# A Mamba and mixture-of-experts block on one core: two buffers for the experts' input, x1 stored early, the gated expert sum accumulated onto it in memory, and a new table of places

## The reference

```python
mod = (_silu(L0_c) @ L0_wmod).reshape(L0_c.shape[0], 6, 1, -1)
sa, ca, ga, sb, cb, gb = (mod[:, 0], ..., mod[:, 5])
ga = (2 * (ga >= 0) - 1) * jnp.maximum(jnp.abs(ga), 0.25)      # gb likewise
h = _layernorm(x) * (1 + ca) + sa
x = x + ga * _L0_attn_ref(h, ...)          # this sum is x1 in the kernel
h = _layernorm(x) * (1 + cb) + sb
x = x + gb * _L0_ffn_ref(h, ...)

def _L0_attn_ref(x, ...):
    h = _rmsnorm(x, norm_w)
    xi, z = split(h @ in_proj_w.T, 2)               # 512 and 512 features
    xi = silu(causal_depthwise_conv(xi, 4 taps) + bias)
    dt, Bm, Cm = split(xi @ x_proj_w.T, [16, 32])   # 16, 16 and 16
    delta = softplus(dt @ dt_proj_w.T + dt_proj_b)
    s = s * exp(delta_t * A) + delta_t * Bm_t * u_t # for each token; 512 x 16 states
    y_t = einsum('bds,bs->bd', s, Cm_t)
    y = (y + u * D) * silu(z)
    return y @ out_proj_w.T + x

def _L0_ffn_ref(x, ...):                            # 16 routed experts, 4 of them per token, and a shared one
    g = sigmoid(x @ gate_w.T); top 4 of 16, normalised -> combine
    routed = sum over e of (silu(x @ e_win[e]) * (x @ e_vin[e]) * combine[e]) @ e_wout[e]
    shared = silu(x @ ws_in) * (x @ vs_in) @ ws_out
    return shared + routed
```

## Time and profile before

| | |
|---|---|
| median of 3 runs | 2980.88 us (2977.16 to 2983.09) |
| profiled execution | 2980.19 us, span in the trace 2978.4 us |
| mean granted clock of TensorE | 0.922 |
| PE (matmul) busy | 2431.5 us, 82% |
| POOL (GpSimd) busy | 2397.0 us, 80% |
| DVE (VectorE) busy | 2277.2 us, 76% |
| ACT (ScalarE) busy | 2129.4 us, 71% |
| moved by DMA | 455.99 MB, 153 GB/s on the mean |

### The profile page before, as it was taken

The page is one execution under the profiler, slowest core; times in us unless marked ns, Lnnn a source line. Parts: engine busy times, 40 slices in busy tenths (PEclk is TensorE's granted clock), DMA queues, the critical chain, the costliest instruction groups (busy, mean ns, idle before and its releaser), DMA issues.

```text
span 2978.4 us, 52216 instructions
## 1 busy us (share of the span) xinstructions
PE 2431.5 (82%) x16084; PEld 1908.7 (64%) x16084; DVE 2277.2 (76%) x3495; ACT 2129.4 (71%) x4033; POOL 2397.0 (80%) x2382
## 2 busy tenths in 40 slices
PE   3557988888797888979888797888979788897879
PEld 1335767667576665757667575766757666676767
DVE  4777778787787878778787877878777787877753
ACT  4786877778686777868677787767868777785641
POOL 1887898889788888888888888888978878897842
PEclk7657999999899999999999899999989999998999
DMA  1775777867676785767677677776757777676841
GB/s 67 195 172 127 167 159 164 179 135 161 147 170 157 165 177 132 163 158 162 155 156 178 138 163 158 156 171 150 167 135 169 160 165 172 135 159 140 179 102 57
DMA packets 154563, 455.99 MB, mean 153 GB/s; under 512 B 22280, under 2 KB 24968, under 8 KB 154032
## 3 DMA queue, kind: packets, MB, share of 16 engines
q0 software_dynamic: 73728, 268.47, 48.2%
q1 hardware_dynamic: 80560, 184.20, 19.9%
HBM read 166.29 MB, written 17.87 MB: 62 GB/s over the span
## 4 chain that ended last, share of the span: by engine, by line
POOL 21%; issue 20%; PE 18%; DVE 15%; ACT 14%; DMA 6%; DVEq 1%; POOLq 0%; ACTq 0%; SPq 0%
POOL db_sb L669 10%; PE bank_ps L1413 8%; DVE states L1150 5%; PE moe_ps L1431 4%; POOL y_sb L681 3%; POOL act L712 3%; DMA y_sb<-c_rows 3%; DMA th_p<-x_dram 3%; ACT c_rows L886 3%; ACT da_ps L913 3%; PE rows_ps L1349 2%; DVE bank_ps L1097 2%; POOL y_sb L690 2%; DVE act L1231 2%; DVE act L1237 1%
## 5 line engine op out<-in xcount | busy, mean ns | idle before, releaser
L669 POOL TENSOR_TENSOR db_sb<-du_sb,b_sb 128x512 f32<-128x512 f32 x1024 | 1575.2, 1710 | 80.3 <-DVE states L1150 79.8
L886 ACT ACTIVATE c_rows<-rows_ps,xd_sb 128x512 f32<-128x512 f32 x1024 | 684.8, 684 | 186.4 <-PE rows_ps L1349 93.9
L1349 PE MATMUL rows_ps<-ident,states 128*128 128x128 f32 x4096 | 646.8, 291 | 177.6 <-ACT c_rows L886 104.9
L913 ACT ACTIVATE da_ps<-delta,a_sb 128x512 f32<-128x512 f32 x1024 | 704.4, 692 | 93.2 <-DVE states L1150 91.5
L712 POOL TENSOR_TENSOR act<-act,w_sb 128x256 f32<-128x256 f32 x512 | 580.8, 1185 | 224.7 <-DMA w_sb<-w_dram 119.4
L681 POOL DMA_DIRECT2D y_sb<-c_rows x512 | 608.2, 1195 | 149.9 <-DMA y_sb<-c_rows 77.1
L1431 PE MATMUL moe_ps<-eout_sb,act 128*128 128x256 f32 x2304 | 621.5, 395 | 103.8 <-POOL act L712 101.6
L1150 DVE TENSOR_TENSOR_SCAN states<-da_ps,carry,db_sb 128x512 f32<-128x512 f32 x512 | 649.3, 1276 | 54.1 <-ACT da_ps L913 52.3
L1349 PEld LDWEIGHTS rows_ps<-ident,states 128*128 128x128 f32 x4096 | 512.6, 150 | 273.8 <-DVE states L1150 123.6
L1413 PE MATMUL bank_ps<-h2T_high,ein_w_high 128*128 128x256 f16 x2304 | 643.2, 279 | 36.0 <-DVE h2T_low L1133 15.0
L1150 DVE TENSOR_TENSOR_SCAN states<-da_ps,db_sb 128x512 f32<-128x512 f32 x512 | 617.4, 1215 | 69.2 <-ACT da_ps L913 68.3
(11 more groups left out here) (169 smaller groups left out, 2633.8 us busy)
## 6 DMA issues: line engine op xcount, KB each, us to landing
y_sb<-c_rows POOLq DMA_DIRECT2D x512, 512.0 KB, 5.5
b_sb<-b_dram SPq DMA_DIRECT2D x128, 512.0 KB, 5.1
w_sb<-w_dram SPq DMA_DIRECT2D x256, 256.0 KB, 4.4
th_p<-x_dram SPq DMA_DIRECT2D x16, 512.0 KB, 8.2
r_dram<-conv SPq DMA_DIRECT2D x16, 512.0 KB, 2.8
x<-r_dram SPq DMA_DIRECT2D x16, 512.0 KB, 5.8
out_dram<-x SPq DMA_DIRECT2D x32, 256.0 KB, 2.3
mod_p<-mod_dram SPq DMA_DIRECT2D x7, 384.0 KB, 11.2
```

What stands on the lines that cost most here:

```text
L669: pool.tensor_tensor(db_sb[:, n % NDB, :], du_sb[:, slots[t][0][0], b, :], b_sb[:, k % NBPAIR, s % BPAIR, :], ALU.mult).then_inc(sem["scal ...
L886: ac.activation(c_rows[:, n % NCR, j % CPAIR, :], rows_ps[j % 2][:, :], ACT.Copy, scale=xd_sb[:, slots[t][0][0], j, s:s + 1]).then_inc(sem ...
L913: ac.activation(da_ps[n % NDA][:, :], delta[:, slots[t][0][0], b, :], ACT.Exp, scale=a_sb[:, b, s:s + 1]).then_inc(sem["exp_done"], 1)
L1349: last = pe.transpose(rows_ps[j % 2][:, b * P:b * P + P], states[:, step % 2 * NB + b, j * P:j * P + P], ident[:, :])
```

## The change

1. **h2T has two buffers**, used in turn by slots[t][2][0]. h2_high waits for the expert_in of the chunk two back, not of the last one.
2. **x1 is stored early.** x1_store writes the whole chunk of x1 to `out` (512 KB) once the four x1 steps are done. It stands on SP behind w_store.
3. **The gated expert sum is accumulated in memory.** out_gate writes moe_ps * gb to SBUF: half 0 into the x1 buffer (free by then), half 1 into the chunk's h2T_high, read as float32. out_join, a DMA issued by GpSimd, adds it to `out` (256 KB each). out_add (VectorE) and out_store (SP) are gone.
4. r_load waits for out_join of half 0 and x1_store, no longer for the last output. mod_m_load loads one row, and mod_g_load, a step of its own, the other (gb) later.
5. `wT` and `weigh` lose their buffers and live in zg; a few waits of a step stand in another order, z_tanh waits for w_stored.
6. **All number tables are new** (SHIFT, PLACE, FIRST, LAST, START, LEAD_*), so nearly every step stands elsewhere by a little.

The diff, cut:

```diff
@@ mix_steps
+    out.append((5.5, ("x1_store", t)))
...
-            out += [(at + 1.75 + TICK, ("out_gate", t, u // NALL)), (at + 1.76 + TICK, ("out_add", t, u // NALL)),
-                    (at + 1.77 + TICK, ("out_store", t, u // NALL))]
+            out += [(at + 1.75 + TICK, ("out_gate", t, u // NALL)), (at + 1.76 + TICK, ("out_join", t, u // NALL))]
...
-LEAD_P0, LEAD_P, LEAD_M = 6.1001, 7.9891, 2.1125
+LEAD_P0, LEAD_P, LEAD_M = -2.6957, 7.9954, 18.0199
...
-    out = [(SLOT * t - 0.95, t, 0, ("mod_m_load", t)) for t in load_mod_m]
+    out = [(SLOT * t - 0.95, t, 0, ("mod_m_load", t)) for t in load_mod_m]
+    out += [(SLOT * t + 20.0, t, 0, ("mod_g_load", t)) for t in load_mod_m]
@@ buffers
-        h2T = [sb(f"h2T_{n}", [P, NK, CH], F16) for n in ("high", "low")]
+        h2T = [sb(f"h2T_{n}", [P, 2, NK, CH], F16) for n in ("high", "low")]
-        wT = sb("wT", [NE, CH])[:, :]
+        wT = zg[0:NE, 1, :]
-        weigh = sb("weigh", [P, NJ, NE])
+        weigh = zg[:, 0, 0:NJ * NE].rearrange("p (j e) -> p j e", j=NJ)
...
+            def gated(t, q):
+
+                if q == 0:
+                    return x1[:, 0:2, :]
+                return h2T[0][:, slots[t][2][0], :, :].rearrange("p k n -> p (k n)").bitcast(F32).rearrange("p (j n) -> p j n", j=2)
@@ SyncE
                     def r_load(t):
...
-                            sp.wait_ge(sem["y_out"], nM(t) * 32)
+                            sp.wait_ge(sem["y_out0"], 16 * nM(t))
+                            sp.wait_ge(sem["x1_out"], 16 * nM(t))
...
-                    def out_store(t, q):
-                        sp.wait_ge(sem["out_added"], 2 * nM(t) + q + 1)
-                        sp.dma_start(out[bass.ds(slots[t][2][1], 1), :, 2 * q:2 * q + 2, :].rearrange("o p j n -> (o p) j n"),
-                                     x1[:, 2 * q:2 * q + 2, :]).then_inc(sem["y_out"], 16)
+                    def x1_store(t):
+
+                        for j in range(NJ):
+                            sp.wait_ge(*bank_read(("op", t, j)))
+                        sp.dma_start(out[bass.ds(slots[t][2][1], 1)].rearrange("o p j n -> (o p) j n"), x1[:, :, :]).then_inc(sem["x1_out"], 16)
@@ GpSimd
+                    def out_join(t, q):
+
+                        pool.wait_ge(sem["out_gated"], 2 * nM(t) + q + 1)
+                        pool.wait_ge(sem["x1_out"], 16 * (nM(t) + 1))
+                        pool.dma_start(out[bass.ds(slots[t][2][1], 1), :, 2 * q:2 * q + 2, :].rearrange("o p j n -> (o p) j n"), gated(t, q),
+                                       accum_op=ALU.add).then_inc(sem[f"y_out{q}"], 16)
@@ ScalarE, h2_high (z_tanh also waits for w_stored, and x_norm's two waits change places)
-                            ac.wait_ge(*bank_full(("expert_in", last, UNITS - 1)))
-                            ac.wait_ge(*bank_full(("expert_in", last, UNITS - 2)))
-                        ac.activation(h2T[0][:, k, :], bank(("h2_t", t, k)), ACT.Copy).then_inc(sem["h2_high_done"], 1)
+                            if nM(t) > 1:
+                                for u in range(UNITS - 2, UNITS):
+                                    ac.wait_ge(*bank_full(("expert_in", last_mix(last), u)))
+                                ac.wait_ge(sem["y_out1"], 16 * (nM(t) - 1))
+                        ac.activation(h2T[0][:, slots[t][2][0], k, :], bank(("h2_t", t, k)), ACT.Copy).then_inc(sem["h2_high_done"], 1)
@@ VectorE
                     def out_gate(t, q):
...
-                        v.tensor_tensor(moe_ps[:, :, :], moe_ps[:, :, :], mod_m[:, 1:2, :].broadcast_to([P, 2, DM]), ALU.mult).then_inc(sem["out_gated"], 1)
-
-                    def out_add(t, q):
-                        v.wait_ge(sem["out_gated"], 2 * nM(t) + q + 1)
-                        place = x1[:, 2 * q:2 * q + 2, :]
-                        v.tensor_tensor(place, place, moe_ps[:, :, :], ALU.add).then_inc(sem["out_added"], 1)
...
+                        v.tensor_tensor(gated(t, q), moe_ps[:, :, :], mod_m[:, 1:2, :].broadcast_to([P, 2, DM]), ALU.mult).then_inc(sem["out_gated"], 1)
```

132 lines of the change are left out of this document (82 added, 50 removed), and 122 rows, old and new, of the table PLACE.

## The result

The changed kernel takes 2948.47 us (median of 4 runs, 2943.24 to 2950.90) against 2981.85 us of the kernel before (median of 4 runs, one more than the table above), a ratio of 0.989 (95% interval 0.987 to 0.991). The prediction was 2955 us. The profiled execution took 2943.24 us, its span is 2941.4 us, 37.0 less than the span before. So the size came out close. The place where the gain is made did not come out as predicted, and the experiments show a part of the change that costs time.

The account below looks back on a forecast made before the run. No engine was the bound, but the order in which four nearly full engines pass work. Per slot -2.9 + 0.4 + 0.9 = -1.6 us; fifteen slots, start -2, end +1 give -25, so 2955 us, own range 2940 to 2970.

Parts of the forecast that it names:

- What shortens the head can shorten the slot; what only spares DVE or POOL in the rest cannot.: Whole slot: a head of some 54 us bound by latencies, then a rest in which PE is nearly full.
- the first w_load: Behind w_store on SP: transfers queued ahead make w_load land 2.8 us later; cost taken as 0.4, between 0 and 2.8.
- the last ends 12.8 us after c_add 15_0 starts: POOL at the slot boundary: the last y_gate ends 12.8 us after c_add 15_0 starts instead of 16.6, 3.8 earlier.
- stands between c_add 15_0 and the first `scaled` of the next slot: POOL at the boundary: out_join of half 1 comes onto POOL there, costing +0.6 us a slot.
- The head, predicted 2.9 us shorter: Start of each slot through the router: 2.3 us shorter at x1_rstd, net -0.6 around the router, 2.9 in all.
- the 2.3 us that I carried from the last y_gate to x1_rstd: Head: about 2.1 of y_gate's 3.8 us survive at x1_rstd; with the 0.8 and +0.6 terms, 2.3 us shorter.
- So logit starts where expert_in started: PE around the router: with xi 1 moved ahead, logit starts at 1322.90 instead of 1324.22, 1.3 us earlier.
- The boundary's transfers: Slot boundary: earlier r_load competes with c_adds, out_join of half 1 replaces out_store; +0.9 us for both, 0 to 2.3 possible.
- rival (a): Slower because the transfers decide: DMA terms at their upper ends, a slot 2.2 us longer, 3012 us; chance 0.25.
- rival (c): More than forecast: new places also close waits priced at nothing; at 3 us per slot 2934 us; chance 0.15.
- my +1 for the end: End of the kernel: accumulating transfer after the last out_gate +2 us, shorter head gives back 1, net +1.
- Start: Before the first slot: x_rstd +3.0 us behind out_scale, conv blocks about 14 instead of 18.5 (-4.5), xd_t -0.5; net -2.

Follow-up runs that it names:

- experiment 3: The changed kernel with out_join of half 1 moved behind the last y_gate of the next slot: 2917.76 us, ratio 0.979 to the kernel before.
- experiment 4: As experiment 3, and r_load also waits for the slot's first scaled: 2891.58 us, ratio 0.970 to the kernel before.
- experiment 5: The changed kernel with w_store issued behind x1_store, r_store and b_load 3: 2939.03 us, ratio 0.986 to the kernel before.
- experiment 2: The kernel before, keeping its old output path, with the change's number tables and the waits these need: 2873.29 us, ratio 0.964 to the kernel before.

## Why the prediction came out as it did

The number was right, 2955 for 2948.5, but by luck: several of its steps were wrong, and the two largest errors went opposite ways.

**Which stretch counts.** The step that failed first is "What shortens the head can shorten the slot; what only spares DVE or POOL in the rest cannot." It was read from PE's 57.71 of 60 us in one window. Over the whole stretch behind the head PE still had 9.5 us of idle time per slot, 5.6 of them waiting for e_weigh, and 3.8 of the 9.5 went away. I should have summed the waits for one kind of instruction over the trace before I called the stretch full. GpSimd's 119.4 us for w_load's data was such a sum, and I had priced the first w_load alone.

**The head.** "the last ends 12.8 us after c_add 15_0 starts" came out as 16.0. The order was read right: with out_join out of the way it is 13.2 (experiment 3). y_gate 0, though, ends 8.4 us behind c_add 15_0 there, for 6.9 before, and z_tanh 2 waits for it. What I had priced at 0.6 us, that out_join "stands between c_add 15_0 and the first `scaled` of the next slot", cost 2.6: the issue and 2.0 of wait a slot for the landing of a c_add. The term was mis-sized by what no row of before showed, a third accumulating transfer behind two (the kernel before never issues one with two under way). The head, predicted 2.9 us shorter, was longer: from c_add 15_0 to the end of h2_low it is 37.3 us for 34.5 before (medians of slots 3 to 14). In experiment 3 it is 34.5 again. So without out_join's wait the head is as long as before, and the 2.3 us that I carried from the last y_gate to x1_rstd and on did not arrive even then.

**logit.** "So logit starts where expert_in started" did not happen. It starts 1.7 us behind the end of h2_low, for 1.4 before (medians). In slot 8 the two xi, 3.1 us together, began 1.5 us ahead of that end, so logit waited for PE itself. Rows of DVE (both h2_low) and PE (the first instruction of xi 0 and of logit):

```profile
1303.21 1.29 DVE L1197 TENSOR_TENSOR h2T_low<-bank_ps,h2T_high 128x512 f16<-128x512 f32 x2 [1.15 <-ACT h2T_high L1021]
...
1302.98 0.63 PE L1360 MATMUL bank_ps<-hnT_high,in_w_high 128*128 128x512 f16 x1
...
1306.12 0.17 PE L1455 MATMUL bank_ps<-gate_w_high,h2T_high 128*128 128x16 f16 x1
```

**The boundary's transfers.** I took +0.9 of 0 to 2.3 for r_load and out_join together. The early r_load and the loads behind it cost 1.7 us a slot alone (experiment 4), out_join's wait 2.0. The bound for the first was right and the value too low, though experiment 4 moved other loads too; the second, GpSimd's own wait, was outside my bounds. Together they are what rival (a) named, 3.7 us a slot for its 2.3 at the boundary; that the time fell all the same is the order's doing, which is rival (c), new places that close waits priced at nothing.

**The first w_load.** The term of 0.4 us of 0 to 2.8 was right to be low: w_load landed 4.6 us later and cost nothing in a slot (experiment 5). But in slot 16, without a preparation, and behind it the burst cost 5.5 us, which my +1 for the end did not have. The end measured -0.2; without the burst it is 5.5 better still.

**Start.** Predicted -2, measured -4.2. x_rstd came 3.06 us later, as predicted (+3.0), the row of GpSimd behind out_scale:

```profile
14.94 1.05 POOL L664 TENSOR_SCALAR out_sb<-out_sb 128x1024 f32<-128x1024 f32 x1 [12.33 <-DMA out_sb<-out_w_dram]
16.06 0.23 POOL L669 TENSOR_SCALAR rstd<-mv 128x4 f32<-128x4 f32 x1
```

But the first tap came only 1.7 us later (38.38 for 36.71), so not all of that delay was passed on. The four conv blocks, from the first tap to the last u, take 12.9 us (38.38 to 51.25) instead of 18.5; 14 were predicted. So the last u ends 4.0 us earlier, nearly the whole 4.2:

```profile
38.38 4.73 DVE L1161 SCALAR_TENSOR_TENSOR bank_ps<-xi_pad,convw_sb,bank_ps 128x512 f32<-128x512 f32 x6
...
49.81 1.44 DVE L1171 SCALAR_TENSOR_TENSOR u_sb<-th_p,bank_ps 128x512 f32<-128x512 f32 x2
```

**Slots 1 and 2.** They gave 11.8 us where my flat rate gave 1.6 for one of them. I had not looked at them apart, and which step counts there was not tried; in experiment 2, on the old output path, they give 14.6 (317.8 for 332.4), so it is the order.

So where -24 were set for fifteen slots, the thirteen from 3 to 15 gave -20.8, and the start with slots 1 and 2 gave -16.0. The forecast of -1.6 us a slot held because two terms of which it had neither nearly cancelled: the order's gain, 6.7 us a slot in experiment 2, and the new path's cost, 4.8, which leave 1.9 by the first scans.

## What to carry to other kernels

When a change brings a mechanism and a newly searched order together, build the two halves apart first; here the order alone is 3.6% faster, the mechanism alone 1.8% slower, and only their sum is a small gain. A wait can be of use: r_load's wait for the last output kept its 512 KB and the modulation rows out of a full stretch, so when a buffer comes free earlier, ask whether the transfer that it allows should start earlier too. Before a stretch is called bound by one engine, sum that engine's waits over all slots, and do not add the waits of its weight loads to those of its matmuls.
